# A decoder layer with a long recurrence on one core: the first block prepared by another split of engines, one expert moved from one side of the scan's end to the other, the scan's last output rows stored later in their queue, and some side jobs placed some steps later

## The reference

```python
# 1. recurrence over 1024 tokens, 16 heads of 16 x 16 state S
q, k, v = silu(x @ Wq), silu(x @ Wk), silu(x @ Wv)
f, gamma = sigmoid(x @ Wf1 @ Wf2), -sigmoid(x @ Wg)
k = k / max(norm(k), 1e-12);  a = k * gamma          # by head
S1 = S + a (k.S);  S2 = f * S1;  S3 = S2 + a (k.S2) + k v;  o = q.S3
out = stack([0, 0, o]) reshaped to 3 * N tokens, the last N kept
out = layernorm(out * sigmoid(x @ Wo1 @ Wo2)) * ln_w @ Wout
# 2. attention of 16 heads on a context of 77 tokens
# 3. experts: x + 2 shared ones + the best 2 of 8 routed ones, exact gelu, width 1024
```

## Time and profile before

| | us |
|---|---|
| median of 3 runs (2336.81 to 2341.67) | 2340.8 |
| the profiled execution's own time | 2338.4 |
| its span, first to last instruction | 2336.6 |
| DVE busy | 2012.8 (86%) |
| PE busy | 1754.3 (75%) |
| POOL busy | 1189.1 (51%) |
| ACT busy | 683.9 (29%) |

### The profile page before, as it was taken

How to read it: one execution, slowest core, us unless ns; L and a number is a source line. 1 busy time by engine, 2 the same in 40 slices (tenths; PEclk the granted TensorE clock), 3 DMA queues, 4 the chain that set the end, 5 groups by cost and what they waited for, 6 DMA issues and landing times.

```text
span 2336.6 us, 33767 instructions
## 1 busy us (share of the span) xinstructions
PE 1754.3 (75%) x10398; PEld 1333.6 (57%) x10398; DVE 2012.8 (86%) x5733; ACT 683.9 (29%) x1363; POOL 1189.1 (51%) x1487
## 2 busy tenths in 40 slices
PE   4258988998789879988998340268887699668993
PEld 2145766676667666766677220145575467555673
DVE  5999999999999999999999998999999989932000
ACT  1132234323432343234323110171223622143120
POOL 2544454565456545654675479473675655222203
PEclk8568999999999999998999765567998689977997
DMA  8100442344234423442345120000254024431353
GB/s 263 42 1 10 140 143 86 107 150 143 84 109 146 143 84 110 148 142 82 108 147 174 44 96 14 21 1 5 102 175 137 1 77 142 135 115 59 108 182 106
DMA packets 175118, 238.65 MB, mean 102 GB/s; under 512 B 28657, under 2 KB 148074, under 8 KB 174954
## 3 DMA queue, kind: packets, MB, share of 16 engines
q1 hardware_dynamic: 140874, 194.46, 24.6%
q10 hardware_dynamic: 27936, 25.44, 3.3%
q0 software_dynamic: 6144, 16.79, 2.2%
HBM read 202.09 MB, written 33.16 MB: 101 GB/s over the span
## 4 chain that ended last, share of the span: by engine, by line
DVE 52%; PE 22%; POOL 10%; issue 7%; ACT 6%; DMA 2%; SPq 0%; POOLq 0%; ACTq 0%; DVEq 0%; PEldq 0%
DVE ps L1610 11%; DVE ps L1591 10%; DVE prod L1583 7%; DVE terms L1598 7%; PE ps L646 4%; DVE terms L1593 4%; PE ps L637 4%; PE ps L582 2%; PE ps L573 2%; DVE rec_out L1537 2%; DVE rec_in L1537 2%; PE ps L519 2%; DVE oprod L1563 2%; ACT eT L847 1%; PE ps L530 1%
## 5 line engine op out<-in xcount | busy, mean ns | idle before, releaser
L1610 DVE TENSOR_REDUCE ps<-terms 128x64 f32<-128x320 f32 x1024 | 449.6, 485 | 0.0
L1591 DVE TENSOR_REDUCE ps<-prod 128x16 f32<-128x272 f32 x1024 | 398.3, 435 | 0.0
L1598 DVE TENSOR_TENSOR terms<-ps,rec_out 128x256 f32<-128x256 f32 x1024 | 382.8, 417 | 0.0
L1583 DVE TENSOR_TENSOR prod<-ps,rec_in 128x256 f32<-128x256 f32 x1024 | 381.9, 416 | 0.0
L637 PE MATMUL ps<-xg,fc 128*128 128x128 f32 x2848 | 351.6, 284 | 27.5 <-PE ps L646 11.9
L637 PEld LDWEIGHTS ps<-xg,fc 128*128 128x128 f32 x2848 | 341.4, 199 | 48.9 <-issue 41.2
L646 PE MATMUL ps<-pj,hT 128*128 128x256 f32 x1424 | 335.0, 389 | 33.2 <-ACT hT L926 33.2
L646 PEld LDWEIGHTS ps<-pj,hT 128*128 128x128 f32 x1424 | 266.3, 192 | 86.4 <-ACT hT L926 52.9
L573 PE MATMUL ps<-xtf,fc 128*128 128x512 f32 x512 | 244.1, 615 | 7.0 <-ACT hT L874 3.7
L582 PE MATMUL ps<-pj,hT 128*128 128x256 f32 x1024 | 238.9, 385 | 0.0
L582 PEld LDWEIGHTS ps<-pj,hT 128*128 128x128 f32 x1024 | 196.4, 193 | 57.5 <-issue 34.4
(11 more groups left out here) (235 smaller groups left out, 3061.0 us busy)
## 6 DMA issues: line engine op xcount, KB each, us to landing
fc<-in_wfcT SPq DMA_DIRECT2D x80, 1024.0 KB, 5.1
pj<-in_wpT SPq DMA_DIRECT2D x80, 1024.0 KB, 7.9
xg_rows<-in_rows ACTq DMA_DIRECT2D x105, 128.0 KB, 2.1
out_rows<-y ACTq DMA_DIRECT2D x89, 128.0 KB, 5.6
in_rows<-o_rows SPq DMA_DIRECT2D x2, 2176.0 KB, 17.4
out_rows<-o_rows SPq DMA_DIRECT2D x2, 2176.0 KB, 17.1
xtp<-in_xT SPq DMA_DIRECT2D x32, 128.0 KB, 2.6
xin<-in_x SPq DMA_DIRECT2D x8, 512.0 KB, 6.6
```

The costliest lines, as they stand in the source:

```text
L1583: tt(prod[:, c % PLACED, :, cols, 0:HD], SE[:, old, cols, 0:HD].unsqueeze(1).to_broadcast([P, NV, HC, HD]), rec_in[:, c].unsqueeze(2).to_b ...
L1591: red(SE[:, old, cols, HD:EH].rearrange("p v n -> p n v"), prod[:, c % PLACED, :, cols, 0:HD + 1], AX.X, ALU.add).then_inc(step_done, 1)
L1598: tt(terms[:, cols, :, 0:NV], SE[:, old, cols, HD:EH].unsqueeze(2).to_broadcast([P, HC, HD, NV]), rec_out[:, c].unsqueeze(1).to_broadcast( ...
L1610: red(SE[:, new, cols, 0:HD], terms[:, cols, :, 0:NV + 1], AX.X, ALU.add).then_inc(step_done, 1)
```

## The change

- First block: its own `prepare_first` on PE projects keys and values in matmuls of 256 columns each, keys ahead of the gate's second matmul and values behind it; ACT applies silu to the keys alone, then the square root to the norms, then the sigmoids, then silu to the values; DVE does the square, sum, floor and a reciprocal where POOL did ten operations; POOL does nothing for this block. The weight w_q is loaded later, w_kv earlier, and the second block's tokens and all that follows them in SP's queue wait for the last projection.
- The context's keys and values are copied out of PSUM by ACT (12 instructions) instead of by DVE (10).
- Tile 6 does expert 8 in its own period and leaves expert 9 alone behind, in the place where expert 8 stood; tile 5 is as it was.
- SP's queue in period 7: the reloads after (6, 6) and (6, 7) stand ahead of the output rows of block 15, and the reload after (6, 8) behind them.
- `BOUND_AT`: divided at 45 instead of 44. `LATER_AT`: minima at 22, 23, 24, 25 instead of 21, 22, 23, 24, resid and 2 at 51 instead of 49, routing at 59 instead of 55.

```diff
@@ -69,7 +69,7 @@
 MOVES = 2 * B
 WEIGHTED = 4
 PREP, PREP_KEPT = 42, 58
-PREP_NORMS, PREP_FIRST = 10, 33
+PREP_FIRST = 27
...
-BEHIND = {False: EXPERTS[LATE:], True: (REST, None, None, REST + 1, None)}
+FREE_REST = EXPERTS[LATE:]
+REST_OF = {FIRST_BOUND: (NE - 2, None, None, NE - 1, None), FIRST_BOUND + 1: (NE - 1, None, None, None, None), LAST: ()}
+
+
+def rest_of(tile):
+
+    return [e for e in REST_OF.get(tile, FREE_REST) if e is not None]
+
+
+def own_of(tile):
+
+    return EXPERTS[NSH:NE - len(rest_of(tile))]
+
+
 STEP = 8
...
@@ -341,10 +353,13 @@
 
                 xt(0)
                 if bound:
-                    used(f, REST)
+                    rest = rest_of(f) if f is not None else []
+                    for e in rest[:-1]:
+                        used(f, e)
                     if load is not None:
                         next_tile(load)
-                    used(f, REST + 1)
+                    for e in rest[-1:]:
+                        used(f, e)
                     outputs(0)
                     used(m, 0)
                     xt(1)
@@ -352,9 +367,15 @@
                         store_tile(f)
                     for e in EXPERTS[1:6]:
                         used(m, e)
-                    outputs(1)
-                    for e in EXPERTS[6:REST]:
+                    if f is None:
+                        outputs(1)
+                    for e in EXPERTS[6:8]:
                         used(m, e)
+                    if f is not None:
+                        outputs(1)
+                    if m != LAST:
+                        for e in own_of(m)[6:]:
+                            used(m, e)
                     return
                 used(f, LATE)
                 if load is not None:
@@ -376,7 +397,7 @@
             sp.sem_inc(o_stored, 1)
             sp.sem_inc(out_stored, 1)
             load_xt(0)
...
-            for dst, src in ((w_f1, wf1), (w_g, wg), (w_kv, wkv), (w_q, wqr)):
+            for dst, src in ((w_kv, wkv), (w_f1, wf1), (w_g, wg)):
                 sp.dma_start(dst[:, :, :], chunked(src)).then_inc(attn_w_in, 16)
             sp.dma_start(w_f2, wf2).then_inc(attn_w_in, 16)
 
@@ -384,9 +405,10 @@
                 sp.dma_start(hT[:, 0:KC, b * SK:(b + 1) * SK], chunked(ctxT[b])).then_inc(ctx_in, 16)
             sp.dma_start(hT[:, 2].rearrange("p (c n) -> p c n", c=KC), chunked(ckT)).then_inc(ctx_in, 16)
             sp.dma_start(hT[:, 3].rearrange("p (c n) -> p c n", c=KC), chunked(cvT)).then_inc(ctx_in, 16)
+            sp.wait_ge(first_ps, 2)
             load_xt(1)
             load_tile(0)
-            for dst, src in ((c_q[:, :, :], cqT), (c_o[:, :, :], coT), (cent[:, :, 0], centT), (cent[:, :, 1], centT), (w_o1[:, :, :], wo1), (w_out[:, :, :], wout)):
+            for dst, src in ((c_q[:, :, :], cqT), (c_o[:, :, :], coT), (cent[:, :, 0], centT), (cent[:, :, 1], centT), (w_o1[:, :, :], wo1), (w_out[:, :, :], wout), (w_q[:, :, :], wqr)):
                 sp.dma_start(dst, chunked(src)).then_inc(xattn_w_in, 16)
...
+            def prepare_first():
+
+                low = LOW[False]
+                xt = [[xtp[:, c].rearrange("p b (n i) -> p i b n", i=CH)[:, i] for c in range(KC)] for i in range(CH)]
+
+                def keys_or_values(half):
+                    for i in range(CH):
+                        for c in range(KC):
+                            ins = mm(ps[:, KV[half], i * D:(i + 1) * D], xt[i][c], w_kv[:, c, half * D:(half + 1) * D],
+                                     start=c == 0, stop=c == KC - 1)
+                    ins.then_inc(first_ps, 1)
+
+                pe.wait_ge(xt_in, 16 * KC)
+                for i in range(CH):
+                    for c in range(KC):
+                        mm(ps[0:HD, low[i], 0:P], w_f1[:, c], xt[i][c], start=c == 0, stop=c == KC - 1)
+                    for c in range(KC):
+                        ins = mm(ps[:, low[i], P:P + H], xt[i][c], w_g[:, c], start=c == 0, stop=c == KC - 1)
+                    ins.then_inc(prep_a_ps, 1)
+                keys_or_values(0)
+                for i in range(CH):
+                    pe.wait_ge(xf1_sb, i * 2 + 2)
+                    mm(ps[:, low[i], D:2 * D], xf1T[:, i], w_f2, start=True, stop=True).then_inc(prep_b_ps, 1)
+                keys_or_values(1)
...
-                last_experts(f, (start, attend, weigh, finish, second), BEHIND[bound])
+                last_experts(f, (start, attend, weigh, finish, second), REST_OF.get(f, FREE_REST))
...
-                    own = EXPERTS[NSH:NE if m == LAST else REST if bound else LATE]
+                    own = own_of(m)
...
             pe.wait_ge(pool_const, 1)
-            pe.wait_ge(attn_w_in, 5 * 16)
-            prepare(0)
+            pe.wait_ge(attn_w_in, 4 * 16)
...
-            pe.wait_ge(xattn_w_in, 10 * 16)
-            pe.wait_ge(ctx_done, KC + 2 * B)
+            pe.wait_ge(xattn_w_in, 11 * 16)
+            pe.wait_ge(ctx_done, KC * QK + 2 * B)
...
+            def prepare_first():
+                low, k, v = LOW[False], vec[:, :, K_COL], vec[:, :, V_COL]
+                for i in range(CH):
+                    act.wait_ge(prep_a_ps, i + 1)
+                    fn(xf1T[:, i], ps[0:HD, low[i], 0:P], ACT.Copy).then_inc(xf1_sb, 1)
+                    fn(graw[:, i], ps[:, low[i], P:P + H], ACT.Copy).then_inc(xf1_sb, 1)
+                act.wait_ge(first_ps, 1)
+                fn(k, ps[:, KV[0], :].rearrange("p (i d) -> p i d", i=CH), ACT.Silu).then_inc(first_k, 1)
+                act.wait_ge(prep_pool, 3)
+                fn(hsum[:, 1], hsum[:, 0], ACT.Sqrt).then_inc(first_root, 1)
+                act.wait_ge(xf1_sb, 2 * CH)
+                fn(beta[:, :, :], graw[:, :, :], ACT.Sigmoid).then_inc(fq_sb, 1)
+                for i in range(CH):
+                    act.wait_ge(prep_b_ps, i + 1)
+                    fn(fbuf[:, i], ps[:, low[i], D:2 * D], ACT.Sigmoid).then_inc(fq_sb, 1)
+                act.wait_ge(first_ps, 2)
+                fn(v, ps[:, KV[1], :].rearrange("p (i d) -> p i d", i=CH), ACT.Silu).then_inc(kv_sb, CH)
+
+            def context():
+
+                act.wait_ge(dve_const, 7)
+                for c in range(KC):
+                    act.wait_ge(ctx_k_ps, c + 1)
+                    for j in range(QK):
+                        fn(keys[:, c, :, j], ps[:, UP + c, 0:B * SK].rearrange("p (b k) -> p b k", b=B), ACT.Copy,
+                           scale=pair_mask[:, j:j + 1]).then_inc(ctx_done, 1)
+                for b in range(B):
+                    act.wait_ge(ctx_v_ps, b // 2 * 2 + 2)
+                    for odd in range(2):
+                        fn(vals[:, b, :, 2 * odd * HD:(2 * odd + 1) * HD],
+                           ps[0:SK, ACC + b // 2, (b % 2) * D:(b % 2 + 1) * D].rearrange("k (h o d) -> k o h d", o=2, d=HD)[:, odd],
+                           ACT.Copy).then_inc(ctx_done, 1)
...
-            prepare(0)
+            prepare_first()
+            context()
             act.wait_ge(pool_const, 1)
-            act.wait_ge(xattn_w_in, 10 * 16)
+            act.wait_ge(xattn_w_in, 11 * 16)
...
-            for i, op in enumerate(preparations(0)[:PREP_NORMS]):
-                prepare(0, i, op)
...
-                done = PREP_NORMS
+                done = 0
...
+                dve.wait_ge(first_k, 1)
+                then(tt(zp[:, :], k, k, ALU.mult))
+                sums(hsum[:, 0])
                 after()
-                dve.wait_ge(fq_sb, CH + 1)
+                then(nc.vector.tensor_scalar(hsum[:, 0], hsum[:, 0], NORM_EPS * NORM_EPS, None, ALU.max))
+                dve.wait_ge(first_root, 1)
+                then(nc.vector.reciprocal(hsum[:, 1], hsum[:, 1]))
+                after()
                 then(tt(heads(vec[:, 0:1, XK_COL]), heads(vec[:, 0:1, K_COL]), by_head(hsum[:, 1, 0:1]), ALU.mult))
-                then(tt(hsum[:, 3], beta[:, :], neg_one[:, :].unsqueeze(1).to_broadcast([P, CH, H]), ALU.mult))
                 after()
                 then(tt(heads(k), heads(k), by_head(hsum[:, 1]), ALU.mult))
+                dve.wait_ge(fq_sb, CH + 1)
+                then(tt(hsum[:, 3], beta[:, :], neg_one[:, :].unsqueeze(1).to_broadcast([P, CH, H]), ALU.mult))
                 after()
                 then(tt(fk[:, :], fbuf[:, :], k, ALU.mult))
...
+                dve.wait_ge(kv_sb, CH)
...
-            dve.wait_ge(dve_const, 7)
-            for c in range(KC):
-                dve.wait_ge(ctx_k_ps, c + 1)
-                tt(keys[:, c], ps[:, UP + c, 0:B * SK].rearrange("p (b k) -> p b k", b=B).unsqueeze(2).to_broadcast([P, B, QK, SK]),
-                   pair_mask[:, :].unsqueeze(1).unsqueeze(3).to_broadcast([P, B, QK, SK]), ALU.mult).then_inc(ctx_done, 1)
-            for b in range(B):
-                dve.wait_ge(ctx_v_ps, b // 2 * 2 + 2)
-                for odd in range(2):
-                    nc.vector.tensor_copy(
-                        vals[:, b, :, 2 * odd * HD:(2 * odd + 1) * HD],
```

(8 more changed lines are left out.)

7 lines of the change are left out of this document (3 added, 4 removed).

## The result

The changed kernel takes 2309.3 us (median of 4 runs, 2308.23 to 2312.74) against 2339.4 us (4 runs of the kernel before, 2336.81 to 2341.67). The ratio is 0.9871, with a 95% interval of 0.9859 to 0.9883: 30.1 us less, where 28.0 were forecast. The span of the profiled execution went from 2336.6 to 2307.7 us, 28.9 less.

The account below looks back on a forecast made before the run. DVE bounds the kernel, busy 86% of the span and 109.82 of 110 us in the scan's first block. Terms 13.9 + 6.8 + 7.3 - 0 = 28.0 us, from 2340.8 to 2312.8; range for 8 in 10: 2306 to 2322.

Parts of the forecast that it names:

- the likeliest case: Whole kernel: the forecast itself, 24 to 31 us saved, 2310 to 2317 us; chance 0.6.
- A: First block: the common part (L1506) starts at 19.65 instead of 33.54, 13.9 us gained; bounds 12 and 15.
- B: Later places in period 7: DVE's waits shrink, 6.8 us gained, two scan chunks of 3.40; between 3.8 and 7.2.
- the store: Output rows behind the expert reloads in SP's queue: loss 0 to 3 us, taken as 0.
- C: End, tile 7: turning follows its norm, router 5.9 earlier, shared expert 1.4 faster; 7.3 us gained, from 4.9 to 10.5.
- Rival 3: First block: table loads with drains or later sigmoids make the gain smaller, 2315 to 2317 us; chance 0.13.
- the drain: ACT, first block: the skill's 1.38 us per switch of table set would make the gain smaller by about 2.3.
- Rival 5: First block starts earlier but DVE waits for something of the second and the gain is given back, 2325 us; chance 0.03.
- Rival 2: Period 7: the later places give nothing, 0 to 2 us gained, 2318 to 2320 us; chance 0.1.
- The danger named: Period 7: places at 63 keep only 6.8 us behind routing for PE's work, which may cost 1 to 3.
- Rival 1: Period 7: reloads hold the queue, output rows come late, 3 to 6 us lost, 2316 to 2319; chance 0.12.
- Rival 4: Behind the router: PE stays at 1.2 GHz after an idle stretch, up to 56 us lost, 2369 us; chance 0.02.

Follow-up runs that it names:

- first_only: Kernel before with only the new first block and the context's copies; experts, SP's order in period 7 and places as before: ratio 0.9939.
- places_only: Kernel before with only the later places of the change: ratio 0.9962 against the kernel before.
- routing_alone: Changed kernel with minima, divided and resid at their old places and only routing later, at 59: ratio 0.9876 against the kernel before.
- expert_only: Kernel before with only the moved expert passes behind the scan and SP's new order of their loads: ratio 0.9969.
- later_still: Changed kernel with further later places, those of period 7 at 65 in the next block: ratio 0.9916 against the kernel before.
- powers_pool: Changed kernel with the first block's norms raised by four powers on POOL instead of ACT's root and DVE's reciprocal: ratio 0.9914 against the kernel before.
- values_first: Changed kernel with the first block's values projected ahead of the gate's second matmul instead of behind it: ratio 0.9891 against the kernel before.
- routing_55: Changed kernel with routing of period 7 back at 55, all other later places kept: ratio 0.9937 against the kernel before.
- later_between: later_still with the output rows of block 15 between the two reloads in SP's queue: ratio 0.9902 against the kernel before.
- store_between: Changed kernel with the output rows of block 15 between the two reloads in SP's queue: ratio 0.9884 against the kernel before.
- none_left: Changed kernel, but tile 6 does expert 9 itself too and leaves none behind: ratio 0.9903 against the kernel before.

## Why the prediction was right, step by step

**Sum.** 28.0 forecast, 28.9 in the profiled execution and 30.1 in the medians; 2309.3 lies in the range. It is 0.7 below the likeliest case's own times (2310 to 2317), while the 30.1 us lie in its 24 to 31: with a fourth run the median before came down from 2340.8 to 2339.4. The terms, as the milestones give them: A 14.1 to 14.5 (13.9 forecast), B 7.1 (6.8), the store -0.6 (0), C 7.9 (7.3).

**First block.** The chain was the right one, down to which wait ends last, the sigmoids'. PE starts at 6.62 instead of 7.1, half a microsecond better and inside the bounds given; the context's copies are on ACT from 21.51 to 26.15, where nothing waits for it; the keys take 3.76 instead of 3.4, the reciprocal 0.35 instead of 0.3, the gates 0.64 instead of 0.81. Rival 3 is out, and with it the drain: the root ends at 16.69, the table load begins at 16.71, and beta stands at 18.00, 0.01 behind the load's end; that is a switch without a drain. (The Trainium skill, "ScalarE: Activation LUTs", section "What ACT_TABLE_LOAD costs", would have had beta no earlier than 20.3, an estimate: from 14.78, two switches of 2.66 and the root's row. The trace decides against it here.) Rival 5 is out, since divided is 14.12 earlier, and first_only's median gained 12.5. That the context's copies cost nothing is read from the rows; no run has them alone.

**Places.** The forecast moved the wait of 2.33 to divided: 2.92 are there (2.77 forecast), none at resid, and 1.93 at routing (2.3). That the stall moves whole hangs on PE's clock as well: in places_only 0.72 was there. Rival 2 is out by places_only and routing_alone. Its converse, that the edits of minima, divided and resid are worth nothing by themselves, which the forecast's sum implied, is shown: they carry 0.9 at most. The danger named, that the places at 63 are too close behind routing, did not come: they stand at 1890.20 without a wait. It is two places later that something breaks, and it is POOL, not PE.

**The loads and the store.** Expert 8's pass ends near 2023.3 in the profile with 9.8 us left, as worked out (9). Rival 1 is out: the last load lands at 2022.52, 7.73 after its issue (8.97 forecast), and the rows are used at 2026.92. The 0.6 more is the size of what profiles differ by. The prediction's sentence that the store can't land before the loads is stronger than what it quotes of the Trainium skill, "DMA: Bandwidth & Descriptors", section "Queues, rings and completion order", an order in which each engine takes up its descriptors. No run here tests it: where the profile has the landing of the loads ahead of the store (the changed kernel, expert_only, later_still, powers_pool), they are down before the rows are used.

**End.** The size was right, its split was not. The step that the turning follows the norm held (6.43 behind DVE, at 1.94 as forecast). The forecast then took 3.46 for the doubling and gave the remaining 1.4 to the shared expert at 7.03. Measured, the clock rose earlier: the doubling took 3.02, the router's own matmuls 1.96 instead of 3.60 before, and the first half of the shared expert took 8.81, no better than the 8.47 of the earlier trace rows. The changed kernel's windows show the clock:

```profile
2108.00:2114.00 6.00, 2.95 (x11) 2.78 (x12) 1.60 (x4) 1.55 (x3) 4.83 (x6) 0.50 0.20 55
2114.00:2121.00 7.00, 7.00 (x29) 4.55 (x28) 2.28 (x13) 2.43 (x3) 4.04 (x5) 0.74 0.36 105
2121.00:2130.00 9.00, 9.00 (x33) 5.41 (x32) 2.62 (x8) 5.00 (x8) 8.40 (x4) 0.95 0.00 0
```

It went up during the doubling, back to 1.2 GHz for some of L620's matmuls, and up again. The forecast's 1.4 for the clock came out as 1.5, and that is luck: 1.9 were won before L620, where it had nothing, and 0.3 lost in it, where it had 1.4 won. Rival 4 is out.

**What the forecast did not see.** Taking the expert away moves POOL's products of the expert rows towards DVE's routing. Before, POOL's gathers waited for the rows of the expert behind finish:

```profile
2142.09 1.05 POOL L1053 DMA_INDIRECT y_back<-out_rows,rows  x1 [11.87 <-ACTq L946]
```

Now they begin right behind the norm, at 2109.45. The products began at 2153.77, 3.7 us behind the choice (L1411 at 2150.04); after, POOL begins at 2121.23, 0.4 behind the choice (L1489 at 2120.82), when DVE is in the very last of its routing operations. The two variants with both experts in their old slots have no long operation there. Of the ten without the expert behind finish, three have none, three (values_first, powers_pool, routing_55) one or two, and four (later_still, later_between, store_between, none_left) four. Four long ones cost 4.6 us in none_left and later_between and 2.1 in later_still and store_between (the column end); one or two cost at most 0.5, since PE is still in the shared expert. Whether some executions of the changed kernel itself fall on the wrong side, one profile can't say. The term "POOL's gathers now fall beside DVE's norm" in the lower bound of C pointed at POOL, but at the wrong pair.

**Open.** In none_left and later_between the router's scores reach ACT 1.4 to 1.5 us later behind the same row of PE (L596, 1.96 in all three traces) than in the changed kernel. PE's ends are modelled; whether these matmuls in fact ran at 1.2 GHz can't be read from the rows.

## What to carry to other kernels

Where one engine is full, follow its waits one by one: a later place wins what the wait behind it holds, up to the next thing that is due, and a place upstream of it wins nothing by itself. Before moving work past a boundary, look at which gap another engine uses there. When a slot is emptied, ask not only what comes earlier but what now runs beside it: here POOL's long products begin 0.4 us behind the choice where they began 3.7 behind it, and in seven of the variants one to four operations of the routing fall beside them and last up to twelve times as long.

## What the runs showed of the hardware

- The same attention of one tile takes 2.5 to 3 us more or less from one kernel to the next, with no edit near it, by when PE's clock rises. Windows of first_only and of the changed kernel over the same work of tile 7:

```profile
2084.00:2093.00 9.00, 7.79 (x84) 6.60 (x84) 1.15 (x1) 4.74 (x9) 3.99 (x2) 0.56 0.01 2
```
```profile
2070.00:2076.00 6.00, 4.77 (x84) 4.07 (x84) 1.18 (x1) 4.59 (x9) 4.02 (x2) 0.94 0.00 0
```

The same 84 matmuls lie in 9 us at 0.56 and in 6 us at 0.94. With several such places in a run, two kernels that differ by less than some 5 us (values_first, store_between, routing_alone and the changed one) can't be told apart by their medians; a stretch within one execution, chosen so that it holds the edit and little else, can do it.
- Two-input operations of DVE on 128x32 took 1.6 to 2.35 us instead of 0.19 beside POOL's on 128x1024, until the end of POOL's; reductions stayed at 0.19; a TENSOR_SCALAR on 128x8 took 1.95 and a CAST on 1x9 2.27.
- Switching ACT between two tables cost its load of 1.28 us and 0.01 to 0.02 around it, here with silu, root and sigmoid in turn.
